# Moving the last eight weight products of the first step behind the second step's first logits, and GpSimd's final sums ahead of its roots

## The chip, the cores and the metric

The kernel runs on one core of a Trainium2 chip. A core has TensorE (PE, matmuls), VectorE (DVE), ScalarE (ACT), GpSimd (POOL) and SyncE (SP), which here only issues DMA transfers. The metric is the device time of one execution in microseconds (us); lower is better. The kernel before takes 1250.19 us (median of three runs).

## What is computed

The reference is two graph layers on N = 2048 nodes with D = 512 features. The first layer is quantised and plays no part in the change. The second builds an attention matrix twice, and this is the part that matters:

```python
Xf, Xa = (X, X)
for s in range(2):
    A = _adj_from_feats(Xa, W1, W2, W3)   # softmax of the logits, top 90% of each row's mass kept, softmax again
    Xf = R @ Xf                           # R: the row-normalised adjacency
    Xa = A @ Xa
    Z = Z + (Xf @ U1s[s] + Xa @ U2s[s])
Y = X + Z                                 # then a layer norm of Y with gamma and beta, added to x
```

`Q @ W2 @ K.T` are the logits, 2048 x 2048; `Q` and `K` are products of `Xa` with small weights.

## The kernel before

The rows of a 2048-row matrix are handled in 16 tiles of 128 rows, in 4 groups of G = 4 tiles; s is the step (0 or 1) and g the group. For a tile of the attention matrix A, DVE searches the threshold that keeps 90% of the mass (passes over `E`, line 1495), collects candidates (1710, 1713), settles the threshold, and writes the kept values as two f16 halves (1718 to 1726). SP then issues four DMA transposes of the tile (line 471, `e_turned`), PE multiplies the transposed chunks by the features (lines 938 and 940: four blocks of 12 matmuls, 128x512, into a PSUM bank AB or RB), and ACT takes the product out of PSUM (1257 in step 0, 1264 in step 1).

Step 0's tile t of `Xa` then goes through its "post" work, which is woven into the next tile: `x_turned` and `x_rest` turn it for use as a stationary operand, into the buffer `XT` by two ACT copies (1104, 1108); `u_product` (14 matmuls, lines 949, 950 and 776, into bank UB) gives the part of Z of this step, which ACT copies to `UO` (1241, `post_out`) and SP stores (442, `z0_store`); `w_product` (12 matmuls of line 776, into bank XB) gives the product with the next step's weight, which ACT copies to `WF` and as a high half to `XHL` (1246, 1249, `w_out`), POOL makes the low half (673), and SP stores both (327, `x_store`). `p_and_k` gives the tile's Q and K; ACT copies them out in five pieces (1114 to 1118, `pk`), POOL makes their low halves (612, 614, `pk_lo`). All of Q and K of step 0's output must be there before step 1's logits begin (PE waits for the semaphore `s_pklo` in `logits`).

The order of each engine's work is written out by hand; `step_order` is the same skeleton for all engines. At its head stands what matters here:

```python
logits(s, 0)
terms(s, 0)
...
for g in range(NG):
    group_start(s, g)
    pairs(s, g)
if s == 0:
    last_post()
```

`logits(1, 0)` on PE is 32 logit matmuls (860, 861) woven with the 32 high-half matmuls of R row 10 (900). On ACT it is the eviction of the logits into `E` (1164) and the squares of two tiles (1171); `terms(1, 0)` is ACT's four exponentials (1201), which DVE's first search pass waits for. R rows are products of the adjacency with the other branch of features (900 and 902, one row is 48 matmuls); ACT and POOL finish them (1224, 1210; 656, 619).

At the very end, group 3 of step 1, SP's `pairs` alternates for each tile: load the stored part of Z (434, `z_in`, into the one buffer ZT, after the sum of the tile before has read it), then issue the transposes of the tile after next. POOL's `pairs` sums `y + ZT` (699) and computes the roots for DVE's layer norms (685): one root for each batch of four finished tiles and one for each of the last four tiles. DVE's order in the end is batch 0, batch 1, tile 12, batch 2, tiles 13, 14 and 15 (1843 to 1853); the root of each waits for the variance that DVE gives (semaphore `s_fvar`).

Of the kernel before, what the change touches and what calls it, by code (L numbers as in the profile page):

```python
# [46 lines left out]
R_FIRST = 9  # L47
R_LATE = 6
R_BEHIND = ((0, 0, 1, 0), (1, 4, 4, 4))
R_HI = 2 * T  # L50
R_ALL = R_HI + T

# [46 lines left out]
def build(nc, x, adjT, scal, w, W1T, W2, W3, U10, U11, U20, U21, gamma, beta, out):  # L99
    ctx = ExitStack()  # L100
    with ctx:
# [162 lines left out]

        def step_order(s, logits, terms, r_one, r_span, group_start, pairs, last_post):
# [26 lines left out]
            return (AB, RB)[(first_use(s, g) + c) % 2]  # L294

        def nothing(s, g):
            pass


        @block.sync  # L300
        def _(sp):
# [160 lines left out]
            def stores(t):  # L462
                x_store(t)
                z0_store(t)
# [84 lines left out]
            step_order(0, nothing, nothing, r_one, r_span, group_start, pairs, last_post)  # L549
            sp.wait_ge(s_uout, 32 * T + OPEN)  # L550
            v_in()
            step_order(1, nothing, nothing, r_one, r_span, group_start, pairs, last_post)
# [6 lines left out]
        def _(pool):  # L559
# [104 lines left out]
                with pool.Fori(a, b) as t:  # L664
                    r_sum(rs, t, rs == 0 and a >= T - R_LATE)

            def post(t, last=False):

                if last:
                    pk_lo(t + T, 1, t, s_wl, t - OPEN)  # L670
# [3 lines left out]
                if not last:  # L674
                    pk_lo(t + T, 1, t, s_wl, t + 1 - OPEN)

            def group_start(s, g):
                if s == 0 and g:
# [8 lines left out]
            def pairs(s, g):  # L687
                for i in range(G):
                    t = g * G + i
                    if s == 0:  # L690
                        if i:
                            post(t - 1)
                        continue
                    if g == NG - 1 and i == 0:
                        root(0, 0, G)
                    y = ends[t % G] if g == NG - 1 else UO
                    pool.wait_ge(s_zin, 16 * t + 16)
                    pool.wait_ge(s_ue, t + 2 * T + 1 + OPEN)
                    q.tensor_tensor(y[:, :], y[:, :], ZT, ALU.add).then_inc(s_y, 1)
                    if g == NG - 1:  # L700
                        if i == 0:
                            root(1, G, 2 * G)
                        root(2 + i + (i > 0), t, t + 1)
                        if i == 0:
                            root(3, 2 * G, 3 * G)

            def last_post():
                post(T - 1, True)

            step_order(0, nothing, nothing, r_one, r_span, group_start, pairs, last_post)  # L710
            step_order(1, nothing, nothing, r_one, r_span, group_start, pairs, last_post)


        @block.tensor
        def _(pe):
# [88 lines left out]

            def x_turned(n):
                pe.wait_ge(s_pkc, T + OPEN)
                pe.wait_ge(s_wf, n - T + OPEN)
                pe.wait_ge(s_xf, n + 1)
                turned(XB, lambda k: XF[:, k * P:(k + 1) * P]).then_inc(s_xT, 1)

            def x_rest(n):
                pe.wait_ge(s_xTh, n - T + 1)
                less(XB, XT[:, 0, :, :].rearrange("p k c -> p (k c)"), minus).then_inc(s_xTs, 1)

            def pk_product(n, bank):

                three(bank[:, 0:P], lambda k: WPK[:, k, 0, :], lambda k: WPK[:, k, 1, :], xh, xl).then_inc(s_pk, 1)

            def post0(n):

# [123 lines left out]
            def u_product(t):  # L944
# [7 lines left out]
                three(UB[:, :], xh, xl, lambda k: UW[:, k, 0, :], lambda k: UW[:, k, 1, :], first=False).then_inc(s_u, 1)  # L952

            def w_product(t):
                three(XB[:, :], xh, xl, lambda k: UV[:, k, 0, :], lambda k: UV[:, k, 1, :]).then_inc(s_w, 1)

            def p_and_k(t):
                pe.wait_ge(s_ue, t + T + 1 + OPEN)
                pk_product(t + T, UB)

            def tile(s, g, i):
# [81 lines left out]
            step_order(1, logits, nothing, r_one, r_span, group_start, pairs, last_post)  # L1043


        @block.scalar
        def _(act):
# [53 lines left out]

            def xT_hi(n):
                act.wait_ge(s_xT, n + 1 + OPEN)
                a(XT[:, 0, :, :].rearrange("p k c -> p (k c)"), XB[:, :], ACT.Copy).then_inc(s_xTh, 1)

            def xT_lo(n):
                act.wait_ge(s_xTs, n - T + 1)
                a(XT[:, 1, :, :].rearrange("p k c -> p (k c)"), XB[:, :], ACT.Copy).then_inc(s_xTc, 1)

            def pk(n, s, t, bank):  # L1110
                i, scale = bass.ts(t, P), SV / (SX * SW)
# [154 lines left out]
            def tile(s, g, i):  # L1266
# [13 lines left out]
                    logits_out(qq + 2 * G, slot, (0, 1))  # L1280
                if post:
                    xT_lo(t - 1 + T)
                    post_out(t - 1)
                    w_out(t - 1)
                if ahead:
# [26 lines left out]
            def last_post():  # L1312
                xT_hi(2 * T - 1)
                xT_lo(2 * T - 1)
                pk(2 * T - 1, 1, T - 1, UB)
                w_out(T - 1)
                post_out(T - 1)

            step_order(0, logits, terms, r_one, r_span, group_start, pairs, last_post)
            step_order(1, logits, terms, r_one, r_span, group_start, pairs, last_post)  # L1320


        @block.vector
# [577 lines left out]
```

## Time and profile before

| | |
|---|---|
| median of three runs | 1250.19 us |
| the three runs | 1252.21, 1250.19, 1250.19 us |
| the profiled execution, its own time | 1250.26 us |
| its span, first to last instruction | 1248.30 us |
| PE busy | 1108.6 us (89%) |
| DVE busy | 1004.0 us (80%) |
| ACT busy | 445.1 us (36%) |
| POOL busy | 282.6 us (23%) |

The profile comes from one execution. Its own time is 1.96 us more than its span. Busy shares are averages over stages with different limits: DVE is idle for tens of microseconds at the seam between the steps, and PE at the end.

### The profile page before, as it was taken

Reading aid. Unit: us, or ns where it says so; the run is one execution under the profiler, and the core shown is the slowest. Engines: PE = TensorE matmul, PEld = TensorE weight load, DVE = VectorE, ACT = ScalarE, POOL = GpSimd, SP = SyncE. Lnnn points to the kernel's source line nnn. Section 1 sums busy time; section 2 is a strip of 40 time slices with the busy share of each in tenths; the row PEclk is TensorE's granted clock in tenths of the full one; section 3 lists DMA queues with packets and bytes.
Section 4 is the critical chain, followed back from the end, with each engine's and each line's share of the span. In section 5 each row is a group of like instructions: output and inputs, shape, how many; then the busy total and the mean of one; then the engine's idle time right before and its main releaser. Section 6 shows DMA issues by size and latency. Waiting matters only on the chain.

```text
span 1248.3 us, 16598 instructions
## 1 busy us (share of the span) xinstructions
PE 1108.6 (89%) x5402; PEld 515.2 (41%) x5402; DVE 1004.0 (80%) x2175; ACT 445.1 (36%) x849; POOL 282.6 (23%) x252
## 2 busy tenths in 40 slices
PE   0578999998999799799899799988899999989794
PEld 0234454554434344344444344433344444434331
DVE  7887777773599998799799201998999999999995
ACT  1764544453733123533423125663043144100000
POOL 6134333343122301211212111322111111111212
PEclk9899999998999999899999899999999999999896
DMA  7154655552234533341461442325673665666445
GB/s 253 49 197 155 199 198 172 193 204 103 92 113 153 160 68 77 76 85 44 122 106 44 102 85 101 127 77 186 191 175 84 170 165 169 179 142 238 117 110 185
DMA packets 190115, 170.62 MB, mean 137 GB/s; under 512 B 144656, under 2 KB 144656, under 8 KB 185936
## 3 DMA queue, kind: packets, MB, share of 16 engines
q1 hardware_dynamic: 190032, 169.66, 47.2%
q8 instruction: 34, 0.56, 0.2%
q14 instruction: 49, 0.40, 0.1%
HBM read 87.31 MB, written 48.76 MB: 109 GB/s over the span
## 4 chain that ended last, share of the span: by engine, by line
DVE 36%; PE 28%; issue 18%; POOL 7%; ACT 5%; DMA 4%; POOLq 1%; SPq 0%; DVEq 0%; ACTq 0%
PE RB L938 5%; DVE WS L1495 5%; PE AB L938 5%; DVE cand L1713 4%; PE UB L776 4%; DVE E L1726 4%; PE XB L776 3%; DVE WS L1710 3%; DVE WS L1718 3%; PE RB L940 3%; DVE g L1575 2%; PE AB L940 2%; DMA AD<-xu_d 2%; DVE E L1468 2%; DVE E L1725 2%
## 5 line engine op out<-in xcount | busy, mean ns | idle before, releaser
L1575 DVE TENSOR_REDUCE g<-E 128x1 f32<-128x2048 f32 x32 | 73.0, 2281 | 102.5 <-ACT E L1164 102.3
L656 POOL TENSOR_TENSOR RT<-RT,AD 128x512 f32<-128x512 f32 x32 | 58.8, 1839 | 286.9 <-ACT RT L1224 286.8
L1495 DVE SCALAR_TENSOR_TENSOR WS<-E,g 128x2048 bf16<-128x2048 f32 x48 | 118.6, 2514 | 0.4
L1713 DVE MAX8 cand<-WS 128x8 f32<-128x128 f32 x512 | 102.1, 277 | 1.1
L673 POOL TENSOR_TENSOR XHL<-WF,XHL 128x512 f16<-128x512 f32 x16 | 24.8, 1553 | 248.0 <-ACT XHL L1249 248.0
L1726 DVE SCALAR_TENSOR_TENSOR E<-WS,E 128x2048 f16<-128x2048 f32 x32 | 78.9, 2466 | 2.3 <-issue 1.2
L1718 DVE SCALAR_TENSOR_TENSOR WS<-E,g 128x2048 f32<-128x2048 f32 x32 | 77.7, 2428 | 0.8
L938 PE MATMUL RB<-XR,turns 128*128 128x512 f16 x256 | 63.6, 393 | 16.3 <-DMA turns<-E 16.3
L1710 DVE SCALAR_TENSOR_TENSOR WS<-E,g 128x2048 f32<-128x2048 f32 x32 | 75.8, 2369 | 1.1
L938 PE MATMUL AB<-VR,turns 128*128 128x512 f16 x256 | 63.8, 394 | 12.9 <-DMA turns<-E 12.9
L938 PE MATMUL AB<-XR,turns 128*128 128x512 f16 x256 | 63.8, 394 | 10.8 <-DMA turns<-E 10.8
L938 PE MATMUL RB<-VR,turns 128*128 128x512 f16 x256 | 62.3, 387 | 10.3 <-DMA turns<-E 10.3
L1201 ACT ACTIVATE E<-E,nmx 128x2048 f32<-128x2048 f32 x32 | 63.7, 1992 | 9.4 <-DVE nmx L1576 9.4
L759 PE MATMUL AB<-E,turns 128*128 128x512 f16 x256 | 59.3, 386 | 5.1 <-DVE E L1396 3.3
L1412 DVE TENSOR_REDUCE E<-E (+1 forms) x16 | 59.4, 3711 | 3.1 <-issue 2.6
L1417 DVE SCALAR_TENSOR_TENSOR turns<-E,turns (+1 forms) x16 | 45.0, 2813 | 21.0 <-ACT turns L1073 21.0
L900 PE MATMUL AB<-VR,turns 128*128 128x512 f16 x256 | 61.5, 379 | 0.0
L900 PE MATMUL AB<-XR,turns 128*128 128x512 f16 x256 | 56.7, 379 | 4.3 <-POOL XR L619 4.3
L766 PE MATMUL AB<-E,turns 128*128 128x512 f16 x256 | 60.3, 379 | 0.0
L900 PE MATMUL RB<-VR,AH 128*128 128x512 f16 x256 | 56.9, 379 | 0.0
L900 PE MATMUL RB<-XR,AH 128*128 128x512 f16 x256 | 56.6, 379 | 0.0
L1725 DVE TENSOR_SCALAR E<-WS 128x2048 f16<-128x2048 f32 x32 | 43.6, 1363 | 14.1 <-issue 11.3
(322 smaller groups left out, 2153.8 us busy)
## 6 DMA issues: line engine op xcount, KB each, us to landing
turns<-adj_parts SPq DMA_DIRECT2D x48, 512.0 KB, 3.8
E<-adjT SPq DMA_DIRECT2D x16, 1024.0 KB, 7.5
adj_parts<-turns SPq DMA_DIRECT2D x16, 1024.0 KB, 5.2
AH<-adj_parts SPq DMA_DIRECT2D x16, 512.0 KB, 4.0
z_d<-UO SPq DMA_DIRECT2D x28, 256.0 KB, 2.3
XR<-x SPq DMA_DIRECT2D x4, 1024.0 KB, 11.8
WS<-U SPq DMA_DIRECT2D x4, 1024.0 KB, 5.5
x_d<-WF SPq DMA_DIRECT2D x16, 256.0 KB, 2.0
```

Of the source, the lines that this page charges most:

```text
L776: i = mm(dst, a(k), b(k), start=(first and n == 0), stop=(last and n == 3 * KC - 1))
L900: i = mm(bank[:, :], at_hi[odd][:, j, :], vs[:, j, k % 2, :], start=(k == 0), stop=False)
L938: mm(bank[:, :], EC[:, c, 0, b, :], xs[:, c * KC + b, y_, :], start=(c + b + y_ == 0), stop=False)
L940: i = mm(bank[:, :], EC[:, c, 1, b, :], xs[:, c * KC + b, 0, :], start=False, stop=(c == NC - 1 and b == KC - 1))
L1201: a(E[:, slot, :], E[:, slot, :], ACT.Exp, bias=nmx[:, slot:slot + 1], accum_out=tot[:, slot:slot + 1]).then_inc(s_exp, 1)
L1495: return v.scalar_tensor_tensor(junk[t % 2], e, g4[:, k, t:t + 1], e, op, ALU.mult, accum_out=g4[:, F_, t:t + 1])
L1575: ct(v.tensor_reduce(row(A2)[:, t:t + 1], E[:, slot, :], AX.X, ALU.max))
L1710: ct(v.scalar_tensor_tensor(WS[:, :], E[:, slot, :], g4[:, U, t:t + 1], E[:, slot, :], ALU.is_lt, ALU.mult, accum_out=g4[:, F_, t:t + 1]))
L1713: i = v.max(cand[:, t, 8 * c:8 * c + 8], WS[:, c * PART:(c + 1) * PART])
L1718: return v.scalar_tensor_tensor(WS[:, :], E[:, slot, :], g4[:, k, t:t + 1], E[:, slot, :], ALU.is_ge, ALU.mult, accum_out=g4[:, DEN, t:t + 1])
L1725: ct(v.tensor_scalar(hi, kept, SE, None, ALU.mult))
L1726: v.scalar_tensor_tensor(lo, kept, SE, hi, ALU.mult, ALU.subtract).then_inc(s_kept, 1)
```

## The change

It has two independent parts. First, `POSTPONED = 12`: for tiles 12 to 15 of step 0, `u_product`, `w_product`, the ACT copies behind them, POOL's low half and SP's two stores leave their places in tiles 13, 14, 15 and `last_post`, and go into a new function `postponed` that each engine calls right behind `logits(1, 0)`. The turned halves of these four tiles can then no longer share the one buffer `XT`; they stand in a free slot of `E` (`x_late`). SP's reload of `XR` (`v_in`) no longer waits for these products. Second, POOL's order in the last group.

```diff
+POSTPONED = T - G
+        x_late = E[:, G, :].bitcast(F16).rearrange("p (t h k c) -> p t h k c", t=G, h=2, k=KC)
+        def x_turned_of(n):
+            return x_late[:, n - T - POSTPONED] if isinstance(n, int) and n >= T + POSTPONED else XT
...
         def step_order(...):
             logits(s, 0)
+            if s and postponed:
+                postponed()
             terms(s, 0)
...
 # SP
-                    if s == 0 and i:
+                    if s == 0 and i and t - 1 < POSTPONED:
                         stores(t - 1)
...
             def v_in():
                 sp.wait_ge(s_vout, 16 * (T - R_LATE) + OPEN)
-                sp.wait_ge(s_u, 2 * T)
+                sp.wait_ge(s_u, T + POSTPONED)
+                sp.wait_ge(s_a, NC * T + OPEN)
...
-            def last_post():
-                stores(T - 1)
+            def postponed():
+                for t in range(POSTPONED, T):
+                    stores(t)
+                sp.wait_ge(s_uout, 32 * T + OPEN)
...
 # POOL
-                    if g == NG - 1 and i == 0:
+                    last = g == NG - 1
+                    if last and i == 1:
                         root(0, 0, G)
-                    y = ends[t % G] if g == NG - 1 else UO
+                    if last and i == 2:
+                        root(1, G, 2 * G)
+                        root(2, T - G, T - G + 1)
+                    if last and i == 3:
+                        root(3, 2 * G, 3 * G)
+                        root(4, T - 3, T - 2)
+                        root(5, T - 2, T - 1)
+                    y = ends[t % G] if last else UO
                     pool.wait_ge(s_zin, 16 * t + 16)
                     pool.wait_ge(s_ue, t + 2 * T + 1 + OPEN)
                     q.tensor_tensor(y[:, :], y[:, :], ZT, ALU.add).then_inc(s_y, 1)
-                    if g == NG - 1:
-                        if i == 0:
-                            root(1, G, 2 * G)
-                        root(2 + i + (i > 0), t, t + 1)
-                        if i == 0:
-                            root(3, 2 * G, 3 * G)
+                    if last and i == 3:
+                        root(6, T - 1, T)
...
 # PE
-                if post:
+                if post and t - 1 < POSTPONED:
                     u_product(t - 1)
                     w_product(t - 1)
...
             def last_post():
-                n = 2 * T - 1
-                x_turned(n)
-                x_rest(n)
-                pe.wait_ge(s_ue, n + OPEN)
-                pe.wait_ge(s_pkc, n + OPEN)
-                pe.wait_ge(s_xTc, n + 1)
-                pk_product(n, UB)
-                w_product(T - 1)
-                pe.wait_ge(s_pkc, n + 1 + OPEN)
-                u_product(T - 1)
+                x_turned(2 * T - 1)
+                x_rest(2 * T - 1)
+                p_and_k(T - 1)
+
+            def postponed():
+                pe.wait_ge(s_pkc, 2 * T + OPEN)
+                pe.wait_ge(s_xTc, 2 * T)
+                for t in range(POSTPONED, T):
+                    pe.wait_ge(s_wf, t + OPEN)
+                    w_product(t)
+                    u_product(t)
...
 # ACT
+            def postponed():
+                for t in range(POSTPONED, T):
+                    w_out(t)
+                    post_out(t)
```

On ACT at the seam between the steps, the rows of the kernel before run like this, from the last piece of Q and K (1118) over tile 15's three copies and the logits (1164) to the squares (1171) and the four exponentials (1201):

```order
L1118 ACTIVATE Khl<-UB 64x128
L1246 ACTIVATE WF<-XB 128x512
L1249 ACTIVATE XHL<-WF 128x512
L1241 ACTIVATE UO<-UB 128x512
L1164 ACTIVATE E,ls<-LB 128x512 x2
L1164 ACTIVATE E,ls<-TB 128x512 x2
...
L1171 ACTIVATE squares,lq<-E 128x1024 x4
L1201 ACTIVATE E,tot<-E,nmx 128x2048 x4
L1224 ACTIVATE RT<-AB,rinv 128x512
```

The same place on ACT in the changed kernel (its line numbers are 40 higher):

```order
L1158 ACTIVATE Khl<-UB 64x128
...
L1204 ACTIVATE E,ls<-TB 128x512 x2
L1211 ACTIVATE squares,lq<-E 128x1024 x4
L1286 ACTIVATE WF<-XB 128x512
L1289 ACTIVATE XHL<-WF 128x512
L1281 ACTIVATE UO<-UB 128x512
...
L1241 ACTIVATE E,tot<-E,nmx 128x2048 x4
L1264 ACTIVATE RT<-AB,rinv 128x512
```

The three copies stand there four times, for tiles 12 to 15. They moved from ahead of the logits to between the squares and the exponentials, so the exponentials now stand behind all four tiles' copies.

On POOL at the very end, group 3 of step 1, the kernel before has these rows (699 are the sums of tiles 12, 13, 14, 15 in this order, 685 the roots; 128x4 is a batch, 128x1 a tile):

```order
L685 TENSOR_TENSOR rstd<-rstd,powc 128x4
L699 TENSOR_TENSOR UO<-UO,Khl 128x512
L685 TENSOR_TENSOR rstd<-rstd,powc 128x4
L685 TENSOR_TENSOR rstd<-rstd,powc 128x1
L685 TENSOR_TENSOR rstd<-rstd,powc 128x4
L699 TENSOR_TENSOR XF<-XF,Khl 128x512
L685 TENSOR_TENSOR rstd<-rstd,powc 128x1
L699 TENSOR_TENSOR RT<-RT,Khl 128x512
L685 TENSOR_TENSOR rstd<-rstd,powc 128x1
L699 TENSOR_TENSOR AD<-AD,Khl 128x512
L685 TENSOR_TENSOR rstd<-rstd,powc 128x1
```

The same place on POOL in the changed kernel (726 the sums, 704 the roots):

```order
L726 TENSOR_TENSOR UO<-UO,Khl 128x512
L704 TENSOR_TENSOR rstd<-rstd,powc 128x4
L726 TENSOR_TENSOR XF<-XF,Khl 128x512
L704 TENSOR_TENSOR rstd<-rstd,powc 128x4
L704 TENSOR_TENSOR rstd<-rstd,powc 128x1
L726 TENSOR_TENSOR RT<-RT,Khl 128x512
L704 TENSOR_TENSOR rstd<-rstd,powc 128x4
L704 TENSOR_TENSOR rstd<-rstd,powc 128x1 x2
L726 TENSOR_TENSOR AD<-AD,Khl 128x512
L704 TENSOR_TENSOR rstd<-rstd,powc 128x1
```

Tile 12's sum (UO) moved ahead of batch 0's root, tile 13's (XF) ahead of the roots of batch 1, tile 12 and batch 2, and tile 14's (RT) ahead of those of batch 2 and tile 13; tile 15's sum (AD) now stands behind the root of tile 14 as it did before.

## Rows read from the trace of the kernel before

**Rows 1.** The page: busy us, share of the span and instructions.
```profile
PE 1108.6 (89%) x5402; PEld 515.2 (41%) x5402; DVE 1004.0 (80%) x2175; ACT 445.1 (36%) x849; POOL 282.6 (23%) x252
```
**Rows 2.** DVE, timeline at the seam: start us, us, operation, idle before and releaser.
```profile
773.86 2.29 DVE L1575 TENSOR_REDUCE g<-E 128x1 f32<-128x2048 f32 x1 [78.60 <-ACT E L1164]
...
793.83 2.35 DVE L1495 SCALAR_TENSOR_TENSOR WS<-E,g 128x2048 bf16<-128x2048 f32 x1
```
**Rows 3.** PE, timeline of one tile's woven products and of the seam.
```profile
716.81 0.38 PE L949 MATMUL UB<-XR,id_sw 128*128 128x512 f16 x1
...
722.42 1.89 PE L938 MATMUL RB<-XR,turns 128*128 128x512 f16 x8
...
764.31 2.75 PE L776 MATMUL XB<-UV,XT 128*128 128x512 f16 x12
...
769.92 0.38 PE L860 MATMUL LB<-Khl,Phh 128*128 128x512 f16 x1
...
783.73 3.62 PE L902 MATMUL AB<-VR,turns 128*128 128x512 f16 x16
```
**Rows 4.** ACT, timeline: tile 15's copy to UO, then the first exponential of step 1.
```profile
770.12 0.60 ACT L1241 ACTIVATE UO<-UB 128x512 f32<-128x512 f32 x1 [1.76 <-PE UB L776]
...
788.73 1.99 ACT L1201 ACTIVATE E<-E,nmx 128x2048 f32<-128x2048 f32 x1
```
**Rows 5.** POOL, timeline: low halves of a stored tile and of K.
```profile
688.96 2.36 POOL L673 TENSOR_TENSOR XHL<-WF,XHL 128x512 f16<-128x512 f32 x1 [4.45 <-ACT XHL L1249]
...
766.46 0.43 POOL L614 TENSOR_TENSOR Khl<-PKf,Khl 64x128 f16<-64x128 f32 x1
```
**Rows 6.** The page, DMA issues: KB each, median us from issue to landing.
```profile
x_d<-WF SPq DMA_DIRECT2D x16, 256.0 KB, 2.0
```
**Rows 7.** PE, timeline: idle times in the second step.
```profile
863.61 0.60 PE L900 MATMUL AB<-XR,turns 128*128 128x512 f16 x2 [4.33 <-POOL XR L619]
...
1180.42 3.57 PE L938 MATMUL AB<-VR,turns 128*128 128x512 f16 x8 [6.44 <-DMA turns<-E]
```
**Rows 8.** SP, timeline at the end: the transposes of tiles 14 and 15.
```profile
1202.85 5.40 SPq L471 DMA_TRANSPOSE turns<-E  x4
...
1223.62 5.32 SPq L471 DMA_TRANSPOSE turns<-E  x4
```
**Rows 9.** PE, timeline at the end: tile 13's last block, tile 15's first.
```profile
1202.54 1.03 PE L940 MATMUL RB<-VR,turns 128*128 128x512 f16 x4
...
1227.38 3.57 PE L938 MATMUL RB<-VR,turns 128*128 128x512 f16 x8 [10.33 <-DMA turns<-E]
```
**Rows 10.** ACT, timeline at the end: tile 12's product taken out.
```profile
1196.35 0.69 ACT L1264 ACTIVATE UO<-AB,rden 128x512 f32<-128x512 f32 x1 [21.64 <-DVE rden L1811]
```
**Rows 11.** POOL, timeline at the end: sums of tiles 12, 13, 14, its root, tile 15 sum.
```profile
1200.80 1.60 POOL L699 TENSOR_TENSOR UO<-UO,Khl 128x512 f32<-128x512 f32 x1
...
1221.57 1.60 POOL L699 TENSOR_TENSOR XF<-XF,Khl 128x512 f32<-128x512 f32 x1
...
1228.54 1.26 POOL L699 TENSOR_TENSOR RT<-RT,Khl 128x512 f32<-128x512 f32 x1
1231.43 1.00 POOL L685 TENSOR_TENSOR rstd<-rstd,powc 128x1 f32<-128x1 f32 x1 [1.64 <-DVE rstd L1846]
1241.44 1.26 POOL L699 TENSOR_TENSOR AD<-AD,Khl 128x512 f32<-128x512 f32 x1 [9.01 <-ACT AD L1264]
```
**Rows 12.** DVE, timeline at the end: layer norms of batches 0 and 1, tiles 13, 14 and 15.
```profile
1199.20 3.74 DVE L1849 SCALAR_TENSOR_TENSOR E<-E,mv,WF 128x512 f32<-128x512 f32 x4
...
1208.63 2.73 DVE L1849 SCALAR_TENSOR_TENSOR E<-E,mv,WF 128x512 f32<-128x512 f32 x4
...
1228.67 1.68 DVE L1853 SCALAR_TENSOR_TENSOR XF<-XF,rstd,XR 128x512 f32<-128x512 f32 x1 [0.52 <-POOL rstd L685]
...
1232.54 0.75 DVE L1853 SCALAR_TENSOR_TENSOR RT<-RT,rstd,XR 128x512 f32<-128x512 f32 x1 [0.52 <-POOL rstd L685]
1242.74 0.69 DVE L1843 BATCH_NORM_STATS2 st<-AD 128x6 f32<-128x512 f32 x1 [9.45 <-POOL AD L699]
```

More of the change, by code:

```diff
@@ L263, in weights_src, with step_order @@
             return u.rearrange("(k p) d -> p k d", p=P)
-        def step_order(s, logits, terms, r_one, r_span, group_start, pairs, last_post):
+        def step_order(s, logits, terms, r_one, r_span, group_start, pairs, last_post, postponed=None):
             logits(s, 0)
+            if s and postponed:
+                postponed()
             terms(s, 0)
@@ L296, in nothing, with no_post @@
         def nothing(s, g):
+            pass
+        def no_post():
             pass
@@ L543, in _ @@
             sp.wait_ge(s_uout, 16 * T + OPEN)
-            def last_post():
-                stores(T - 1)
+            def postponed():
+                for t in range(POSTPONED, T):
+                    stores(t)
+                sp.wait_ge(s_uout, 32 * T + OPEN)
             at_lo_in(0, 0)
             ad_in(0, 0)
-            step_order(0, nothing, nothing, r_one, r_span, group_start, pairs, last_post)
-            sp.wait_ge(s_uout, 32 * T + OPEN)
+            step_order(0, nothing, nothing, r_one, r_span, group_start, pairs, no_post)
             v_in()
-            step_order(1, nothing, nothing, r_one, r_span, group_start, pairs, last_post)
+            step_order(1, nothing, nothing, r_one, r_span, group_start, pairs, no_post, postponed)
             sp.wait_ge(s_rout, 16 * T + OPEN)
@@ L665, in r_span, with w_lo @@
                     r_sum(rs, t, rs == 0 and a >= T - R_LATE)
-            def post(t, last=False):
-                if last:
-                    pk_lo(t + T, 1, t, s_wl, t - OPEN)
+            def w_lo(t):
                 pool.wait_ge(s_wf, t + 1 + OPEN)
@@ L673, in post @@
                 q.tensor_tensor(XHL[:, 1, :], WF[:, :], XHL[:, 0, :], ALU.subtract).then_inc(s_wl, 1)
-                if not last:
-                    pk_lo(t + T, 1, t, s_wl, t + 1 - OPEN)
+            def post(t):
+                if t < POSTPONED:
+                    w_lo(t)
+                pk_lo(t + T, 1, t, s_wl, min(t + 1, POSTPONED) - OPEN)
+            def postponed():
+                for t in range(POSTPONED, T):
+                    w_lo(t)
             def group_start(s, g):
@@ L699, in pairs @@
                     q.tensor_tensor(y[:, :], y[:, :], ZT, ALU.add).then_inc(s_y, 1)
-                    if g == NG - 1:
-                        if i == 0:
-                            root(1, G, 2 * G)
-                        root(2 + i + (i > 0), t, t + 1)
-                        if i == 0:
-                            root(3, 2 * G, 3 * G)
+                    if last and i == 3:
+                        root(6, T - 1, T)
             def last_post():
-                post(T - 1, True)
+                post(T - 1)
             step_order(0, nothing, nothing, r_one, r_span, group_start, pairs, last_post)
-            step_order(1, nothing, nothing, r_one, r_span, group_start, pairs, last_post)
+            step_order(1, nothing, nothing, r_one, r_span, group_start, pairs, last_post, postponed)
         @block.tensor
@@ L812, in x_rest, with halves_turned @@
                 pe.wait_ge(s_xTh, n - T + 1)
-                less(XB, XT[:, 0, :, :].rearrange("p k c -> p (k c)"), minus).then_inc(s_xTs, 1)
+                less(XB, x_turned_of(n)[:, 0, :, :].rearrange("p k c -> p (k c)"), minus).then_inc(s_xTs, 1)
+            def halves_turned(n):
+                return [lambda k, h=h: x_turned_of(n)[:, h, k, :] for h in range(2)]
             def pk_product(n, bank):
-                three(bank[:, 0:P], lambda k: WPK[:, k, 0, :], lambda k: WPK[:, k, 1, :], xh, xl).then_inc(s_pk, 1)
+                hi, lo = halves_turned(n)
+                three(bank[:, 0:P], lambda k: WPK[:, k, 0, :], lambda k: WPK[:, k, 1, :], hi, lo).then_inc(s_pk, 1)
             def post0(n):
@@ L951, in u_product @@
                 pe.wait_ge(s_xTc, n + 1)
-                three(UB[:, :], xh, xl, lambda k: UW[:, k, 0, :], lambda k: UW[:, k, 1, :], first=False).then_inc(s_u, 1)
+                hi, lo = halves_turned(n)
+                three(UB[:, :], hi, lo, lambda k: UW[:, k, 0, :], lambda k: UW[:, k, 1, :], first=False).then_inc(s_u, 1)
             def w_product(t):
-                three(XB[:, :], xh, xl, lambda k: UV[:, k, 0, :], lambda k: UV[:, k, 1, :]).then_inc(s_w, 1)
+                hi, lo = halves_turned(t + T)
+                three(XB[:, :], hi, lo, lambda k: UV[:, k, 0, :], lambda k: UV[:, k, 1, :]).then_inc(s_w, 1)
             def p_and_k(t):
-                pe.wait_ge(s_ue, t + T + 1 + OPEN)
+                if t < POSTPONED:
+                    pe.wait_ge(s_ue, t + T + 1 + OPEN)
+                else:
+                    pe.wait_ge(s_ue, POSTPONED + T + OPEN)
+                    pe.wait_ge(s_pkc, t + T + OPEN)
+                    pe.wait_ge(s_xTc, t + T + 1)
                 pk_product(t + T, UB)
@@ L1030, in last_post @@
             def last_post():
-                n = 2 * T - 1
-                x_turned(n)
-                x_rest(n)
-                pe.wait_ge(s_ue, n + OPEN)
-                pe.wait_ge(s_pkc, n + OPEN)
-                pe.wait_ge(s_xTc, n + 1)
-                pk_product(n, UB)
-                w_product(T - 1)
-                pe.wait_ge(s_pkc, n + 1 + OPEN)
-                u_product(T - 1)
+                x_turned(2 * T - 1)
[8 more added lines that the diff above has]
+                    u_product(t)
             step_order(0, logits, nothing, r_one, r_span, group_start, pairs, last_post)
-            step_order(1, logits, nothing, r_one, r_span, group_start, pairs, last_post)
+            step_order(1, logits, nothing, r_one, r_span, group_start, pairs, last_post, postponed)
         @block.scalar
@@ L1282, in tile @@
                     xT_lo(t - 1 + T)
+                if post and t - 1 < POSTPONED:
                     post_out(t - 1)
@@ L1315, in last_post, with postponed @@
                 pk(2 * T - 1, 1, T - 1, UB)
-                w_out(T - 1)
-                post_out(T - 1)
+            def postponed():
+                for t in range(POSTPONED, T):
+                    w_out(t)
+                    post_out(t)
             step_order(0, logits, terms, r_one, r_span, group_start, pairs, last_post)
-            step_order(1, logits, terms, r_one, r_span, group_start, pairs, last_post)
+            step_order(1, logits, terms, r_one, r_span, group_start, pairs, last_post, postponed)
         @block.vector
```

10 lines of the change are left out of this document (7 added, 3 removed).

## The prediction

> **What bounds the kernel now.** I read the busy shares first [rows 1]: DVE is busy for 80% of the span and PE for 89%, so neither is the bound everywhere, and the question is which of them the end waits for in each of the two places that the change touches. The chain that ended last, followed in order of time, runs over PE up to the seam between the steps (tiles 12 to 15 of step 0 and their woven products), then over DVE through all of step 1, and ends over one POOL sum, one set of transposes and PE's last tile.
>
> At the seam the timeline of DVE shows why: DVE sits idle for 78.60 us until ACT has written the first logits of step 1 [rows 2]. PE works almost without a break in that time, so whatever PE does there ahead of the logits delays DVE by its full length. From 793.83 us, the first search pass, DVE never waits for another engine again until the last tiles. PE on the other hand waits for DVE: 6.44 us at the first tile of the last group [rows 7].
>
> At the end the timeline shows a second hole. PE waits 10.33 us for the transposes of tile 15 [rows 9]. SP could not issue them before 1223.62 [rows 8], because its queue stood at the load of ZT that waits for tile 13's sum, and that sum ran on POOL only at 1221.57 [rows 11], though PE had finished tile 13 at 1203.57 [rows 9]. In between POOL stood at roots, waiting for variances from DVE.
>
> **The change at the seam.** One tile's products take PE from 716.81 to 722.42 [rows 3], 5.61 us. Three such sets leave the stretch before `last_post`: 3 x 5.61 = 16.8 us. The fourth set (764.31 to 769.92, again 5.61 [rows 3]) leaves too, but it was cover: meanwhile ACT copied tile 15's Q and K and POOL made their low halves, done at 766.46 + 0.43 = 766.89 [rows 5]. PE must wait for that before the first logit, so of the fourth set only 769.92 - 767.0 = 2.9 us is won, and about 2.7 us of it becomes a wait. The logits begin 16.8 + 2.9 = 19.7 us earlier, at 750.2. I expect no new limit in the shortened tiles: without the products a tile has 11.7 us on PE, and four transposes take SP 5.40 us [rows 8]. SP's stores leave its queue there too, and the row product woven into the logits needs nothing new. The logits end, and row 10's low half could begin, at 783.73 - 19.7 = 764.0 [rows 3].
>
> Those 19.7 us are not DVE's gain. DVE's search pass needs an exponential, and the changed order of ACT puts all twelve copies of the four postponed tiles between the squares and the first exponential. The copies follow PE: 4 x 5.61 = 22.4 us of products from 764.0 to 786.4, with perhaps 0.1 us for the first hand-over, since ACT must first finish its squares (now at 788.73 - 19.7 = 769.0 at the latest [rows 4]). The last copy starts 0.2 us after its product, as it did before (770.12 against 769.92 [rows 3, 4]), and takes 0.60; so the first exponential begins at about 787.2, ends 2 us later [rows 4], and DVE starts its first pass at about 789.4 instead of 793.83 [rows 2]. **Gain 4.4 us.** DVE's work ahead of it (maxima, moments) ends 19.7 us earlier, at 774, and then DVE idles 15 us. Each later exponential takes 2.0 us and a pass 2.35, so the others are in time.
>
> PE does the same work in another order and has lost 2.7 us to the new wait, so it enters R row 10's low half 2.7 us later than before, at about 786.5. Does it hold DVE up? The 4.33 us that PE idled in the R row of 863.61 [rows 7] came from ACT, which stood in exponentials paced by DVE; with DVE 4.4 us earlier that supply comes at 859.2 and PE, 2.7 us late, needs it at 862.0: that idle time goes, and PE is some 1.6 us ahead from there. Were nothing of it won, PE would be 2.7 us late and DVE 4.4 early against a slack of 6.44 at the last group [rows 7], a loss of 0.7 us; I take none. SP's queue: eight stores and the wait for their landing now stand ahead of the loads for R rows 11 and 12. They end about 2.5 us after the last product (0.6 copy, 2.0 landing [rows 6]), at 789; row 12's load is needed two R rows later (20.7 us of PE from 783.73 before), so about 7 us stay after its own landing of 4. POOL's four low halves fall where DVE idles.
>
> **The change at the end.** All times here are as if the last group still began at the old time; the 4.4 us come on top. ACT has tile 12's product in UO at 1196.35 + 0.69 = 1197.0 [rows 10]. POOL now sums at once, from 1197.1 to 1198.7 (1.60 [rows 11]) instead of from 1200.80; SP issues tile 14's transposes from 1199.1 (before 1202.85 [rows 8]), the last of them when tile 13's last block is done at 1203.57 [rows 9], and PE goes on into tile 14 with no gap, to about 1213.9. Tile 13's sum comes right behind its eviction, at 1204.4 to 1206.0, 17 us earlier than 1221.57 [rows 11]; tile 15's transposes follow tile 14's blocks, and PE ends tile 15 at about 1224.3, where it only started at 1227.38 before [rows 9].
>
> So PE leaves the path and DVE takes it. Tile 15's sum on POOL stands behind the root of tile 14, which cannot run before DVE has tile 14's variance: 1231.43, done 1232.43 [rows 11]. The sum takes 1.26 more [rows 11]: 1233.7. DVE finishes tile 14 at 1232.54 + 0.75 = 1233.3 [rows 12] and starts tile 15's norm at 1233.75 instead of 1242.74 [rows 12]. **That is 9.0 us** by durations as they stand.
>
> They will not quite stand. Where a sum ran on POOL, DVE's two-input operation beside it took longer: the four of batch 0 took 3.74 us with tile 12's sum among them, those of batch 1 2.73 with none, a difference of 1.0; tile 13's took 1.68 with tile 14's sum beside it against 0.75 for tile 14's [rows 12], 0.93. Three sums hit DVE so before. Now tile 12's falls under the one-input statistics (1196.2 to 1198.7) and should cost nothing, tile 13's falls at the end of batch 0 (0 to 1), tile 14's runs against tile 12's last operation (0.9), tile 15's against tile 14's (0.9, of which 0.45 was waiting anyway). The three old costs of 1.0, 1.0 and 0.93 go. Net 2.9 - 0.9 - 0.5 - (0 to 1) = 0.5 to 1.5 us more. I take 1.0: **gain at the end 10.0 us**, bounds 8.5 (every sum costs DVE a full 1.0) and 10.5.
>
> The Trainium skill, page "SBUF — State Buffer", section "Who interferes with whom", says that a DVE instruction with two SBUF inputs contends with a GpSimd instruction that reads SBUF, that the one which starts second fully blocks, and that one with a single input does not contend. By that rule a sum could cost DVE up to its whole 1.3 to 1.6 us, which speaks against packing four sums beside DVE; the rows above show 0.93 to 1.0 each, and the rows decide. With 1.6 for each of three sums the end would gain some 7 us.
>
> **Sum.** 4.4 + 10.0 = 14.4 us. The profiled execution took 1250.26 us, its span 1248.30 plus 1.96 around it, and the median of the runs is 1250.19, 0.07 less. The span becomes 1233.9 and the time 1235.8; I say 1236.0.
>
> **The rivals.** (a) *The seam gives nothing, the end does*: about 1240. The four tiles' copies run through single buffers (XHL, UO), each reused only when its store has landed. The loop is ACT 0.6, POOL up to 2.36 [rows 5], issue 0.3, landing 2.0 [rows 6]: 5.3 us, just under the 5.61 of PE's products. With 1.1 us more per tile the 4.4 us are gone. For it: the margin is thin if POOL runs at its slow value. Against: POOL is slow beside DVE's long operations, and DVE idles there. Chance 0.12.
>
> (b) *Slower than before*: the same loop with landings so slow that DVE's first pass comes after 793.8 + 10.0 = 803.8, which eats the end's gain as well. The products would have to end 14.4 us later, 3.6 us per tile, a cycle of 9.2 us against 5.61. A landing of 6 us instead of 2.0 would do it; the decision point is there, and at 10.5 us a cycle the time would be 1255. The reload of XR, 2.5 MB, is issued before the logits now and done before the first store, so I see nothing in these queues that makes a landing three times as long. Chance 0.03.
>
> (c) *DVE gets all of the 19.7 us*: were the exponentials not held by the copies, DVE's chain would move by 19.7, until PE, whose work is the same and whose idle time is 6.44 at the last group [rows 7] plus the smaller pieces before it, became the bound after some 16 us. Time 1250.2 - 16 - 10 = 1224. Against it speaks the written order on ACT. Chance 0.03.
>
> (d) *The end gains less*, some 5 us, because transposes, the load of the last x1 tiles and the outputs share the DMA engines and PE's last tile comes after POOL's root: it would have to be over 8 us late (1224.3 against 1232.4). Time 1241. Chance 0.07.
>
> **The numbers.** The forecast (both gains, 1233 to 1239) has 0.75. The range has to take in the seam between 2 and 6 us and the end between 8.5 and 10.5, which gives 1233.5 to 1239.5, and reach into (a): 1232.5 to 1240.0. A measurement tells from no change what is beyond 0.2%, 2.5 us. Faster: forecast, (a), (c), (d) and most of what I have not thought of, 0.95; same 0.02; slower 0.03.
>
> **What would show it.** DVE's first maximum at about 754 and its first pass at 789, with some 15 us idle between them; PE in eight sets of products from 764 to 786.5 without gaps; a PE wait of 2.7 us before the first logit; the first exponential right behind the fourth copy to UO; PE without its 10.33 us wait at the end; tile 15's sum directly behind tile 14's root, and DVE's wait before tile 15 under 1 us. The prediction is wrong if the copies' cycle is over 5.6 us, if PE is the engine waited for at the last group (its 6.44 us gone), or if DVE's operations at the end are longer by more than 1 us for each sum.

## The result and the profile after

The changed kernel takes 1236.3 us (median of four runs, 1235.5 to 1237.7) against 1250.2 (median of four, 1246.2 to 1252.2). The recorded ratio is 0.9904, interval 0.9889 to 0.9919; the medians just given would make it 0.9889, at the edge of that interval, while with the kernel before's median of 1248.2 us in 15 later runs it is 0.9904. The profiled execution took 1235.52 us, its span 1233.6. The forecast was 1236.0 us, faster than before.

The page of the changed kernel, its busy shares and its chain (the lines of [rows 1]):

```profile
PE 1104.6 (90%) x5402; PEld 514.4 (42%) x5402; DVE 1006.7 (82%) x2175; ACT 445.0 (36%) x849; POOL 280.1 (23%) x252
...
DVE 37%; PE 26%; issue 18%; POOL 7%; DMA 5%; ACT 4%; SPq 1%; POOLq 1%; DVEq 0%; ACTq 0%
```

DVE's timeline at the seam, which answers to [rows 2] (start us, us, operation, idle before and releaser):

```profile
752.95 2.29 DVE L1619 TENSOR_REDUCE g<-E 128x1 f32<-128x2048 f32 x1 [59.44 <-ACT E L1204]
...
773.34 1.15 DVE L1659 TENSOR_TENSOR g<-g 128x4 f32<-128x4 f32 x1
788.19 2.35 DVE L1539 SCALAR_TENSOR_TENSOR WS<-E,g 128x2048 bf16<-128x2048 f32 x1 [13.70 <-ACT E L1241]
```

The first maximum comes 20.9 us earlier by the times of the two traces, the first search pass only 5.6: in between DVE now waits 13.70 us for the exponential. ACT's timeline shows what the exponential stood behind (with [rows 4]): tile 13's copies wait 0.69 us for a store to land, and tile 15's last copy directly precedes the exponential.

```profile
772.54 0.63 ACT L1289 ACTIVATE XHL<-WF 128x512 f16<-128x512 f32 x1 [0.69 <-DMA x_parts<-XHL]
...
785.50 0.60 ACT L1281 ACTIVATE UO<-UB 128x512 f32<-128x512 f32 x1 [1.76 <-PE UB L799]
786.00 1.99 ACT L1241 ACTIVATE E<-E,nmx 128x2048 f32<-128x2048 f32 x1
```

PE's timeline there, with [rows 3]: tile 12's first block, the first logit, the first postponed product, and row 10's low half behind the last one. The 22.48 us from 762.82 to 785.30 are the eight products.

```profile
691.66 3.57 PE L968 MATMUL AB<-XR,turns 128*128 128x512 f16 x8 [7.29 <-DMA turns<-E]
...
746.39 0.61 PE L890 MATMUL LB<-Khl,Phh 128*128 128x512 f16 x1 [2.47 <-POOL Khl L628]
746.80 0.63 PE L891 MATMUL LB<-Khl,Plz 128*128 128x512 f16 x1
...
752.46 0.38 PE L890 MATMUL LB<-Khl,Phh 128*128 128x512 f16 x1
...
762.82 2.75 PE L799 MATMUL XB<-UV,E 128*128 128x512 f16 x12
...
785.30 3.62 PE L932 MATMUL AB<-VR,turns 128*128 128x512 f16 x16
```

Two things stand here that the forecast did not have. Tile 12 began 4.15 us earlier than in the trace before (691.66 against 695.81), ahead of everything the change touches. And behind the wait of 2.47 us the first logit matmuls take 0.61 to 0.63 us each instead of 0.38, and the woven logits together take 16.4 us (746.39 to 762.82) instead of 13.8.

At the end, POOL and DVE (with [rows 11, 12]); first POOL's sums of tiles 12, 13, 14 and 15:

```profile
1192.09 1.27 POOL L726 TENSOR_TENSOR UO<-UO,Khl 128x512 f32<-128x512 f32 x1 [19.04 <-ACT UO L1304]
...
1198.57 1.51 POOL L726 TENSOR_TENSOR XF<-XF,Khl 128x512 f32<-128x512 f32 x1 [2.83 <-ACT XF L1304]
...
1211.10 1.26 POOL L726 TENSOR_TENSOR RT<-RT,Khl 128x512 f32<-128x512 f32 x1
...
1226.30 1.26 POOL L726 TENSOR_TENSOR AD<-AD,Khl 128x512 f32<-128x512 f32 x1
```

And DVE's batch 0, tiles 12, 13, 14, and the start of tile 15:

```profile
1191.11 2.47 DVE L1887 BATCH_NORM_STATS2 st<-E 128x6 f32<-128x512 f32 x4
...
1194.11 2.74 DVE L1893 SCALAR_TENSOR_TENSOR E<-E,mv,WF 128x512 f32<-128x512 f32 x4
1196.88 3.75 DVE L1897 SCALAR_TENSOR_TENSOR E<-E,rstd,UW 128x512 f32<-128x512 f32 x4
...
1211.23 1.67 DVE L1897 SCALAR_TENSOR_TENSOR UO<-UO,rstd,XR 128x512 f32<-128x512 f32 x1 [0.51 <-POOL rstd L704]
...
1223.50 0.75 DVE L1897 SCALAR_TENSOR_TENSOR XF<-XF,rstd,XR 128x512 f32<-128x512 f32 x1 [0.51 <-POOL rstd L704]
...
1226.43 1.67 DVE L1897 SCALAR_TENSOR_TENSOR RT<-RT,rstd,XR 128x512 f32<-128x512 f32 x1 [0.51 <-POOL rstd L704]
1228.02 0.68 DVE L1887 BATCH_NORM_STATS2 st<-AD 128x6 f32<-128x512 f32 x1
```

From the statistics of batch 0 to those of tile 15 it is 36.9 us, where it was 46.5 (1196.20 to 1242.74). DVE no longer waits ahead of tile 15. PE waits 0.20 us ahead of tile 14 and not at all ahead of tile 15, where it waited 10.33 [rows 9].

### The profile page after: what moved, and what is told of

Same layout as the page of the kernel before. It is cut to its first block, busy times and chain, and to the rows that moved or that the text cites. A ratio compares the mean times of both kernels' runs of the same rounds, so it can differ in the third digit from the quotient of the medians.

```text
span 1233.6 us, 16608 instructions
## 1 busy us (share of the span) xinstructions
PE 1104.6 (90%) x5402; PEld 514.4 (42%) x5402; DVE 1006.7 (82%) x2175; ACT 445.0 (36%) x849; POOL 280.1 (23%) x252
## 4 chain that ended last, share of the span: by engine, by line
DVE 37%; PE 26%; issue 18%; POOL 7%; DMA 5%; ACT 4%; SPq 1%; POOLq 1%; DVEq 0%; ACTq 0%
DVE WS L1539 5%; PE RB L968 5%; DVE cand L1757 4%; PE AB L968 4%; PE UB L799 4%; DVE E L1770 3%; PE XB L799 3%; DVE WS L1754 3%; DVE WS L1762 3%; DVE g L1619 2%; PE RB L970 2%; PE AB L970 2%; DVE E L1769 2%; DMA AD<-xu_d 2%; DVE E L1512 2%
## 5 line engine op out<-in xcount | busy, mean ns | idle before, releaser
L670 POOL TENSOR_TENSOR RT<-RT,AD 128x512 f32<-128x512 f32 x32 | 52.5, 1639 | 271.0 <-ACT RT L1264 270.9
L726 POOL TENSOR_TENSOR UO<-UO,Khl 128x512 f32<-128x512 f32 x13 | 24.3, 1867 | 139.9 <-ACT UO L1304 136.5
```

## The experiments

Three stretches of each trace are compared, since they stay clear of what varies elsewhere: from PE's first block of tile 12 to DVE's first search pass (the seam), from there to the first statistics of batch 0, and from these to tile 15's statistics (the end). Times are in us and from one profiled execution each; the ratios, with 95% intervals, are against the kernel before, run beside each.

| kernel | tile 12 begins | seam | search to batch 0 | end | ratio (interval) |
|---|---|---|---|---|---|
| before | 695.81 | 98.0 | 402.4 | 46.5 | 1 |
| before, once more | 695.92 | 98.2 | 402.1 | 45.0 | |
| end only | 692.61 | 98.5 | 403.9 | 35.9 | 0.9918 (0.9898 to 0.9939) |
| seam only | 692.68 | 96.4 | 402.9 | 45.7 | 0.9976 (0.9962 to 0.9990) |
| changed | 691.66 | 96.5 | 402.9 | 36.9 | 0.9904 (0.9889 to 0.9919) |
| changed, filler in the wait | 692.13 | 94.0 | 402.4 | 36.9 | 0.9887 (0.9863 to 0.9910) |
| changed, tile 12's product in the wait | 696.52 | 91.0 | 405.5 | 35.9 | 0.9860 (0.9838 to 0.9883) |
| changed, exponentials woven | 690.77 | 82.7 | 402.4 | 36.9 | 0.9805 (0.9790 to 0.9821) |
| all three edits | 691.08 | 79.5 | 400.3 | 37.0 | 0.9763 (0.9749 to 0.9776) |

**The end alone.** The kernel before, with POOL's new order in the last group as the diff above has it.

> The kernel before with the new order of POOL's sums and roots alone; the seam is as before. Theory A (what the trace of the changed kernel shows: from the last group's rden to the start of tile 15's norm it is 9.6 us shorter): the time falls by 9.6 us, to a ratio of 0.992, and tile 15's norm starts 36.9 us after the first statistics of batch 0 instead of 46.5. Theory B (the end gains less by itself, because in the changed kernel the earlier seam also moved the loads and stores of the end): less than 8 us, ratio above 0.9935.

Measured: 1238.3 us against 1248.2, ratio 0.9918, so some 10 us; the end stretch is 35.9 us. Theory A holds: the end's gain does not need the seam. That the stretch is 1.0 us shorter than the 36.9 us of the changed kernel has a reason in the trace. Tile 13's sum falls here beside statistics of DVE, which keep their 2.47 us, and not beside the last operation of batch 0, which took 3.75 us in the changed kernel and takes 2.74 here:

```profile
1200.71 2.74 DVE L1857 SCALAR_TENSOR_TENSOR E<-E,rstd,UW 128x512 f32<-128x512 f32 x4
1203.13 1.45 POOL L707 TENSOR_TENSOR XF<-XF,Khl 128x512 f32<-128x512 f32 x1 [3.57 <-ACT XF L1268]
1203.37 2.47 DVE L1847 BATCH_NORM_STATS2 st<-E 128x6 f32<-128x512 f32 x4
```

**The seam alone.** The changed kernel with this old order put back on POOL, in place of the lines that the diff above adds there:

```diff
+                    if g == NG - 1 and i == 0:
+                        root(0, 0, G)
                     y = ends[t % G] if g == NG - 1 else UO
...
+                    if g == NG - 1:
+                        if i == 0:
+                            root(1, G, 2 * G)
+                        root(2 + i + (i > 0), t, t + 1)
+                        if i == 0:
+                            root(3, 2 * G, 3 * G)
```

> The changed kernel with POOL's old order at the end, so only the seam is changed. Counted from PE's first block of tile 12 in step 0, DVE's first search pass of step 1 came after 98.0 us before and after 96.5 us in the changed kernel. Theory A (the wait of 2.5 us ahead of the first logit let the granted clock fall and cost another 2.6 us; the 4 us by which the changed kernel's trace already led at tile 12 vary between executions): the time falls by 1 to 2 us, ratio 0.9984 to 0.9992, and the interval may include 1. Theory B (the seam gives the 4.4 us of the prediction): ratio 0.9965. Theory C (the 4 us ahead of tile 12 belong to the change as well): ratio 0.9955.

Measured: 1245.2 us against 1248.2, ratio 0.9976. The interval (0.9962 to 0.9990) leaves out theory C's 0.9955. It takes in theory B's 0.9965 and most of theory A's 0.9984 to 0.9992, so the time does not tell A from B. The trace does: the seam stretch is 96.4 us, 1.6 to 2.1 less than in the three traces whose seam is the old one. Theory B's 4.4 us are not there. Another 0.8 us came at the end by DVE's and POOL's timing (45.7 against 46.5), which is within what the kernel before itself varies by there (45.0).

**The kernel before once more**, unchanged, for its trace.

> The kernel before once more, for its trace. Theory A (what differs ahead of tile 12 is variation between executions): PE's first block of tile 12 begins anywhere from 691 to 697 us, not at 695.8 again; the first search pass 98 us after it. Theory B (the change itself moved it): 695.8 within 0.5 us.

Measured: tile 12 at 695.9, and the first search pass 98.2 us after it. By itself the start is what theory B said, and theory A had said that it would not be 695.8 again. The other traces speak against B: "end only" has the program of the kernel before up to the last group and began tile 12 at 692.6, and one of the kernels with the changed seam began it at 696.5. So starts near 692 and near 696 occur with either seam. The two kinds already part at tile 8: in the three traces that start near 696, PE waits 3.06 to 3.20 us ahead of tile 8 and its first eight matmuls then take 3.43 to 3.57 us; in the six others it waits 1.49 to 2.16 us and they take 1.89. The time of the changed kernel says the same. From tile 12 to the end its trace is 10.6 us shorter, which the recorded interval (10.1 to 13.9 us of 1248.2) takes in, while the 14.7 us between the spans are outside it. With nine traces it is not shown that the change has no part at all in how often the early start occurs.

**A filler in the wait.** Tile 12's weight product is computed once more, for no use, where PE waits ahead of the logits:

```diff
                 p_and_k(T - 1)
+                hi, lo = halves_turned(T + POSTPONED)
+                three(XB[:, :], hi, lo, lambda k: UV[:, k, 0, :], lambda k: UV[:, k, 1, :])
```

> The changed kernel, with twelve matmuls of no use (tile 12's weight product, computed a second time later and overwritten) in the place where PE waits for the last low half of K. No work is taken from elsewhere. Theory A (the wait itself let the clock fall): the clock stays at full speed, the woven logits take 13.8 us instead of 16.4, and the first search pass comes 93.9 us after tile 12's first block instead of 96.5; the time falls by 2.6 us against the changed kernel. Theory B (the logits were slow because their PSUM banks or ACT held them): they still take 16.4 us and nothing is gained.

Measured: seam 94.0 us against 96.5, as theory A said; ratio 0.9887 (0.9863 to 0.9910) against 0.9904 (0.9889 to 0.9919). The two intervals overlap, so it is the stretch that shows the gain, and the whole times only agree with it. Stretches of the changed kernel (columns: busy us of PE, PEld, DVE, ACT, POOL with their counts, granted clock, DMA share, GB/s): ahead of the logits, their first 6.6 us, and the rest.

```profile
738.00:746.30 8.30, 3.74 (x35) 2.33 (x33) 0.00 (x0) 4.36 (x13) 1.66 (x4) 0.91 0.62 229
746.30:752.90 6.60, 6.50 (x19) 2.44 (x20) 0.00 (x0) 2.73 (x8) 0.04 (x1) 0.59 0.30 111
752.90:762.80 9.90, 9.90 (x47) 4.49 (x46) 7.75 (x7) 7.80 (x24) 0.00 (x0) 1.00 0.00 0
```

The same stretches with the filler:

```profile
738.00:746.30 8.30, 6.12 (x48) 3.52 (x46) 0.00 (x0) 4.35 (x13) 1.23 (x3) 1.00 0.62 205
746.30:752.90 6.60, 6.60 (x32) 2.87 (x31) 2.05 (x1) 4.30 (x13) 0.46 (x2) 1.00 0.38 142
```

In the same 6.6 us PE starts 19 matmuls at a granted clock of 0.59 and 32 at 1.00. The wait cost twice: its own 2.5 us, and 2.6 us more afterwards. Twelve matmuls without use made the seam 2.5 us shorter. The filler ends the wait and adds work in one, so which of the two kept the clock up is not told apart here.

**Tile 12's product in the wait.** The same place, but with work that is needed anyway:

```diff
 # PE, last_post
                 p_and_k(T - 1)
+                w_product(POSTPONED)
 # PE, postponed
-                    pe.wait_ge(s_wf, t + OPEN)
-                    w_product(t)
+                    if t > POSTPONED:
+                        pe.wait_ge(s_wf, t + OPEN)
+                        w_product(t)
                     u_product(t)
 # ACT, last_post
                 pk(2 * T - 1, 1, T - 1, UB)
+                w_out(POSTPONED)
 # ACT, postponed
-                    w_out(t)
+                    if t > POSTPONED:
+                        w_out(t)
                     post_out(t)
```

> The changed kernel, with tile 12's weight product (12 matmuls, 2.6 us) and its copy out of the bank moved from behind the logits into PE's wait ahead of them, where they are useful. Theory A: the wait and the slower clock go, and 2.6 us less stand between the logits and the first exponential: first search pass 91.3 us after tile 12's first block instead of 96.5, time 5.2 us less than the changed kernel, about 1231, unless PE, which gains the same 5.2 us, is not in the way later. Theory B (the clock has another cause): 2.6 us at most.

Measured: seam 91.0 us, ratio 0.9860, which is 5.5 us less than the changed kernel's 0.9904 of 1248. Theory A holds, with a reserve: the seam is 5.5 us shorter in the trace too, but the stretch from the search to batch 0 is 2.6 us longer there (405.5 against 402.9), most of it idle time of DVE for which the profile names no releaser. The profiled execution was the slowest of the five. PE's timeline there has the product, the first logit right behind it with no idle time in brackets, and the transposes behind the last logit, 13.8 us after the first:

```profile
748.29 2.75 PE L799 MATMUL XB<-UV,E 128*128 128x512 f16 x12
750.92 0.39 PE L890 MATMUL LB<-Khl,Phh 128*128 128x512 f16 x1
...
764.74 0.38 PE L979 MATMUL UB<-XR,id_sw 128*128 128x512 f16 x1
```

**The exponentials woven between the copies.** `terms(1, 0)` returns at once, and its four exponentials are called from `postponed` on ACT:

```diff
                 for t in range(POSTPONED, T):
                     w_out(t)
+                    if t == POSTPONED + 1:
+                        terms(1, 0, (1,), True)
+                    if t == POSTPONED + 2:
+                        terms(1, 0, (3,), True)
                     post_out(t)
+                    if t == POSTPONED:
+                        terms(1, 0, (0,), True)
+                    if t == POSTPONED + 1:
+                        terms(1, 0, (2,), True)
```

> The changed kernel with ACT's four exponentials of step 1's first group taken from behind all copies of the four postponed tiles into the gaps between them (behind tile 12's copies, between tile 13's, behind them, between tile 14's). Theory A (the exponentials' place held DVE, which idles 13.7 us ahead of its first search pass, and PE has idle time further on that can go): the first pass comes 83 us after tile 12's first block instead of 96.5, and as DVE now leads PE by some 14 us the bound becomes PE; its waits of 5.8 us at the last group and some 3.5 us in the group before go, with the slower clock behind each: 8 to 12 us less than the changed kernel, 1224 to 1228. Theory B (PE, busy without a break from 885 us on, sets the time already): DVE only waits elsewhere, and nothing is gained. Theory C (ACT's delay of tile 13's and 14's copies stalls PE): the products take over 23 us instead of 22.5.

Measured: 1222.8 us, ratio 0.9805, 12.4 us less than the changed kernel (0.0099 of 1248); seam 82.7 us. DVE's first pass starts at 773.49 where it was 788.19. Theory C falls: PE's products run from 761.78 to 784.26, 22.48 us, as before. Theory B falls too. PE's waits for transposes at the last group, first in the changed kernel, then here:

```profile
1175.35 3.36 PE L968 MATMUL AB<-VR,turns 128*128 128x512 f16 x8 [5.78 <-DMA turns<-E]
```

```profile
1159.98 1.89 PE L968 MATMUL AB<-VR,turns 128*128 128x512 f16 x8 [1.45 <-DMA turns<-E]
```

The wait of 3.65 us that the changed kernel has one group earlier (at 1104.32) is gone altogether. PE had this idle time to give, and with 1.45 us left here PE and DVE are nearly even.

**All three edits.** The two edits above, and on POOL `root(4, ...)` and `root(5, ...)` moved behind tile 15's sum:

```diff
                     if last and i == 3:
                         root(3, 2 * G, 3 * G)
-                        root(4, T - 3, T - 2)
-                        root(5, T - 2, T - 1)
                     y = ends[t % G] if last else UO
...
                     if last and i == 3:
+                        root(4, T - 3, T - 2)
+                        root(5, T - 2, T - 1)
                         root(6, T - 1, T)
```

> The changed kernel with three edits: tile 12's weight product and its copy ahead of the logits, the exponentials woven between the copies, and tile 15's sum on POOL ahead of the roots of tiles 13 and 14. Theory A: PE gains the 5.2 us of the first edit and the waits named for the second; 13 to 18 us less than the changed kernel, 1218 to 1223; and DVE's last operation of tile 14 takes 0.75 us instead of 1.67, as the sum no longer runs beside it. Theory B (PE's order of R rows and tiles is the bound from 885 us on): only the 5 us of the first edit.

Measured: 1217.4 us, ratio 0.9763, 17.6 us less than the changed kernel and 5 less than with the exponentials alone. That is the best kernel here. Its PE waits from 760 us on, in total, times, longest:

```profile
PE RB L932 <- DMA turns<-adj_parts: 3.9, 2, 3.3
PE LB L890 <- ACT E L1206: 2.0, 1, 2.0
PE AB L968 <- ACT XF L1308: 0.8, 1, 0.8
```

No wait for the transposes of E is left, and over a long stretch of step 1 PE is busy throughout (columns as in the stretches above), where the changed kernel's PE is busy for 280.92 of the same 285.00 us:

```profile
885.00:1170.00 285.00, 285.00 (x1322) 129.22 (x1321) 271.83 (x686) 70.71 (x137) 44.55 (x26) 1.00 0.64 167
```

So PE is now the bound there. The third edit gave nothing at the end. Tile 14's last operation takes 0.75 us as expected, but the end stretch is 37.0 us as before, since the sum now runs beside the last operations of batch 2 and lengthens them (3.74 us, which were 2.74 in the changed kernel):

```profile
1198.35 3.74 DVE L1911 SCALAR_TENSOR_TENSOR E<-E,rstd 128x512 f32<-128x512 f32 x4
...
1207.22 0.75 DVE L1911 SCALAR_TENSOR_TENSOR RT<-RT,rstd,XR 128x512 f32<-128x512 f32 x1 [0.52 <-POOL rstd L704]
```

## Why the prediction was right, and where it was not

The time was right to 0.3 us, but the two terms were not equally right, and part of the agreement is luck.

**The end, forecast 10.0 us.** The stretch shrank by 9.6 us in the changed kernel and the time of "end only" fell by some 10. Each step came as told: the sums of tiles 12 and 13 at 1192.09 and 1198.57 are 5.0 and 5.8 us ahead of the forecast's 1197.1 and 1204.4, of which 5.1 is that the last group began earlier; PE lost its 10.33 us; tile 15's sum follows tile 14's root, and DVE goes on without a wait. The correction for sums beside DVE was right too: tile 12's sum fell under the statistics and cost nothing (2.74 us for line 1893, which was 3.74 [rows 12]), tile 14's and tile 15's cost 0.92 each (1.67 against 0.75). Tile 13's cost a full 1.0 (3.75 against 2.74), the upper of the two bounds, and with that the forecast's own sum gives 9.5. In "end only" it fell beside statistics and cost nothing. The Trainium skill, page "SBUF — State Buffer", section "Who interferes with whom", says that an operation of DVE with two inputs in SBUF contends with one of GpSimd that reads SBUF, and that one with a single input, outside its 2-port modes, does not; the rows agree. The page calls the shared port pair an exclusive lock, and that the one which starts second fully blocks it says of DVE's 2-port modes. The rows do not settle whether that holds here: tile 14's and tile 15's sums, of 1.26 us, each began 0.13 us before DVE's operation, which leaves up to 1.13 us to block, and 0.92 were measured.

**The seam, forecast 4.4 us.** The traces give 1.5 to 2 (98.0 to 98.5 became 96.4 to 96.5), the time of "seam only" 3.0 with an interval from 1.2 to 4.7. The mechanism was right: the logits came early, the exponentials stood behind the copies, and the products took 22.48 us where 22.4 were told, with ACT, POOL and the stores in step, so rival (a)'s slow loop did not occur. The step that was mis-sized is "about 2.7 us of it becomes a wait". The wait was 2.47 us, but it was counted at its own length only. The granted clock fell to its lower level (1.2 of 2.4 GHz) about 1 us into the wait and came back 5.3 us behind the first logit (granted 0.50 from 744.9 to 751.7), and the logits took 2.6 us more. 4.4 - 2.6 = 1.8 us; the two traces show 1.5, since the logits also began 19.4 us earlier, counted from tile 12, and not 19.7. The length of the wait would not have told this. The kernel before waits 2.96 us at 1203.57, and the changed kernel 2.46 us at 811.37, and both go on at full speed:

```profile
1206.53 1.89 PE L938 MATMUL AB<-VR,turns 128*128 128x512 f16 x8 [2.96 <-DMA turns<-E]
```

```profile
813.83 0.39 PE L890 MATMUL LB<-Khl,Phh 128*128 128x512 f16 x1 [2.46 <-ACT E L1204]
```

In both places PE had worked without a gap before. Ahead of the logits the wait stands behind three others (0.20, 1.21 and 0.78 us), and of 8.3 us, the wait included, PE was busy for 3.74.

**What made the sum fit.** 9.6 and some 1.5 to 3 us are 11 to 13; the profiled pair differs by 14.7, since 4.15 us of it lie ahead of tile 12 and 0.5 was lost in between. By the recorded ratio the gain is 12.0 us (10.1 to 13.9), and the 14.4 of the forecast lie just outside. The kernel before ran from 1245.4 to 1251.7 in 15 later runs, with a median of 1248.2 instead of 1250.2. The median of three runs against which the forecast was made was a high one, by about 2 us, and this made up for the term that was too large. The range has a slip of 0.2 us, which changes nothing: gains of 2 and 8.5, and of 6 and 10.5, taken from 1250.2 give 1239.7 and 1233.7, not 1239.5 and 1233.5.

**The claim on PE.** That PE would not hold DVE up was right, with 5.78 us left at the last group, though PE entered row 10's low half 5.7 us later than before, counted from tile 12, and not 2.7: the slow logits delayed it too. The idle time at R row (1, 0) went as told, but at the next row PE waited 5.03 us for its low half instead of 3.98. Rival (c), DVE with all of the seam's gain, was built as "exponentials woven": the forecast of 1224 for that case was met with 1222.8, and PE does become nearly even with DVE.

## What to carry to other kernels

Work that is postponed behind an early result must be postponed on every engine: here PE's products moved behind the logits, but their copies moved ahead of the next thing that the bound engine waits for, and 14 of 20 us stayed there until the exponentials were put between them. When cover is taken away from a wait, price the wait and the clock behind it, and look for a piece of the moved work that can stay as cover. At a queue that waits for a helper engine's result, order the helper's work by when its inputs are ready, and see which operations it then runs beside: the same sum cost 1.0 us beside one and nothing beside another. Try each part of a change alone, because two terms of 10 and 2 us can add up to a forecast of 14 by luck.

## What the runs showed of the hardware

A wait of 2.47 us on TensorE, behind three short ones, was followed by 5.3 us at the lower clock (0.50); with twelve matmuls of no use in that place the clock stayed full (1.00) and the seam was 2.5 us shorter. Waits of 2.96 and 2.46 us out of steady work were not followed by a lower clock. The Trainium skill, page "TensorE: Matmul & The Clock Gate", section "Part 1: The HAM clock gate (the "warmup" mystery)", says that idleness brings the throttled state back; the rows agree, and they show that the length of one wait alone does not tell.

Executions of one program differ by up to 8.0 us here (1228.41 to 1236.45 in five runs of one kernel, 1245.35 to 1251.67 in 15 of the kernel before). Across nine traces of eight kernels tile 12's first block begins at 690.8 to 696.5 us, with nothing between 692.7 and 695.8, and whether it is early or late goes with the wait ahead of tile 8: 1.49 to 2.16 us with the full clock behind it, or 3.06 to 3.20 us with the lower one. The start of tile 8 itself already varies, from 611.5 to 615.9 us; what makes it so was not tried.
